# Attention activations and outputs turned by transposing transfers, and the early heads of a long convolution reordered, in a one-core decoder layer

## The reference, cut to what matters

```python
# 1: attention with quantized linear layers (16 heads of 32)
def _act_quant(x):
    s = 127.0 / jnp.clip(jnp.max(jnp.abs(x), axis=-1, keepdims=True), 1e-05)
    return jnp.clip(jnp.round(x * s), -128.0, 127.0) / s
...
qkv = _bitlinear(_layernorm(x), w_qkv)
attn = softmax(causal(einsum('bnhd,bmhd->bhnm', q, k) * SCALE))
x = x + _bitlinear(einsum('bhnm,bmhd->bnhd', attn, v), w_proj)
# 2: long convolution per head (32 heads of 8 channels), gated by ctx
kv = vr[:, :, :, None, :] * x2r[:, :, None, :, :]
y = irfft(rfft(kv, n=2 * L) * k_f)[..., :L] + kv * skip
x = x + einsum('bhijl,bhil->bhjl', y, x1r)
# 3: gated feed-forward on fp8-rounded weights
x = x + down(silu(gate(ln(x))) * up(ln(x)))
```

## Time and profile before

| | |
|---|---|
| median of 3 runs | 1532.92 us (1530.36 to 1533.33) |
| profiled execution | 1535.45 us, its span 1533.7 us |
| PE, DVE, POOL, ACT busy share of the span | 93%, 85%, 74%, 49% |
| attention in steady state | about 123 to 419 us |
| heads 0 to 4 | 494.9 to about 600 us |
| convolution and feed-forward together | from about 610 us |

### The profile page before, as it was taken

One profiled execution on the slowest core, in us unless ns is written; L12 is line 12 of the kernel. 1 busy time (PEld: TensorE's weight loads), 2 busy tenths in 40 slices (PEclk: granted clock), 3 DMA queues, 4 the chain that ended last, 5 costly groups with the idle time before them and its releaser, 6 DMA issues.

```text
span 1533.7 us, 24061 instructions
## 1 busy us (share of the span) xinstructions
PE 1433.5 (93%) x8717; PEld 808.9 (53%) x8717; DVE 1308.0 (85%) x2018; ACT 745.4 (49%) x1334; POOL 1132.6 (74%) x818
## 2 busy tenths in 40 slices
PE   3589999999986988999999999999999999999998
PEld 2477888788763443444444444444444444444443
DVE  5789999999875789899999999999899999999611
ACT  3589999999884112333233333333333334323231
POOL 2379999999984777767776777767866877777432
PEclk9799999999997999999999999999999999999999
DMA  3555555564613422010201300310220121020000
GB/s 140 140 135 152 146 151 157 139 168 128 155 48 97 149 69 67 23 41 25 72 21 35 83 21 21 81 36 22 55 62 21 38 59 42 18 72 1 7 21 28
DMA packets 89218, 113.12 MB, mean 74 GB/s; under 512 B 38133, under 2 KB 42381, under 8 KB 89101
## 3 DMA queue, kind: packets, MB, share of 16 engines
q1 hardware_dynamic: 88908, 111.45, 26.1%
q10 hardware_dynamic: 192, 0.14, 0.1%
HBM read 50.67 MB, written 19.92 MB: 46 GB/s over the span
## 4 chain that ended last, share of the span: by engine, by line
PE 52%; DVE 26%; issue 8%; ACT 7%; POOL 6%; DMA 1%; DVEq 0%; POOLq 0%; SPq 0%; ACTq 0%
PE gu L745 12%; PE gu L759 10%; PE shared_bank L690 6%; DVE y L1110 6%; DVE z L1112 4%; POOL pL L1606 2%; PE y L709 2%; PE y L706 2%; DVE fu L1131 2%; PE y L714 2%; PE y L715 2%; DVE kv L1080 2%; PE gu L704 2%; PE y L712 2%; DVE blockmax L874 2%
## 5 line engine op out<-in xcount | busy, mean ns | idle before, releaser
L1492 ACT ACTIVATE shared<-shared_bank 128x512 f32<-128x512 f32 x162 | 96.6, 596 | 422.6 <-PE shared_bank L690 422.6
L1110 DVE TENSOR_TENSOR y<-shared,y 128x512 f32<-128x512 f32 x324 | 223.9, 691 | 6.8 <-PE y L715 1.2
L1606 POOL TENSOR_TENSOR pL<-pT,pH 128x768 f16<-128x768 f32 x128 | 216.6, 1694 | 12.8 <-ACT pH L1319 5.3
L1732 POOL TENSOR_TENSOR fuL<-fu,fuH 128x512 f16<-128x512 f32 x96 | 121.1, 1262 | 115.9 <-ACT fuH L1507 115.9
L1116 DVE TENSOR_REDUCE oT<-z 128x64 f32<-128x512 f32 x256 | 175.6, 686 | 8.8
L745 PE MATMUL gu<-fT,wu 128*128 128x512 f16 x768 | 183.0, 381 | 0.0
L745 PE MATMUL gu<-fT,wg 128*128 128x512 f16 x768 | 181.4, 379 | 0.0
L1112 DVE TENSOR_TENSOR z<-y,cT 128x512 f32<-128x512 f32 x236 | 162.4, 688 | 11.9 <-PE y L704 6.3
L1678 POOL TENSOR_TENSOR kv<-vT,cT 128x1024 f32<-128x1024 f32 x70 | 148.5, 2123 | 6.9 <-ACT vT L1485 5.5
L759 PE MATMUL gu<-wd,fuH 128*128 128x512 f16 x384 | 145.5, 379 | 0.0
L759 PE MATMUL gu<-wd,fuL 128*128 128x512 f16 x384 | 145.5, 379 | 0.0
(11 more groups left out here) (208 smaller groups left out, 3529.7 us busy)
## 6 DMA issues: line engine op xcount, KB each, us to landing
pack<-qkhl SPq DMA_DIRECT2D x256, 128.0 KB, 2.4
x_sb<-in_x SPq DMA_DIRECT2D x16, 512.0 KB, 4.3
c_sb<-in_ctx SPq DMA_DIRECT2D x32, 256.0 KB, 3.5
hankel<-in_L_xattn_k SPq DMA_DIRECT2D x32, 256.0 KB, 4.0
out_y<-yo SPq DMA_DIRECT2D x32, 256.0 KB, 2.8
x_grp<-x_scratch SPq DMA_DIRECT2D x30, 256.0 KB, 3.5
x_scratch<-x_sb SPq DMA_DIRECT2D x14, 512.0 KB, 2.8
wraw<-in_L_attn_w_qkv SPq DMA_DIRECT2D x3, 1024.0 KB, 9.8
```

What stands on the lines that cost most here:

```text
L1110: chain.step(V.tensor_tensor(bank[:], shared[2 * part + half][:], bank[:], op))
L1606: G.tensor_tensor(pL[n % 2][:], pT[n % NP][:], pH[n % NP][:], ALU.subtract).then_inc(low_done, 1)
L1732: G.tensor_tensor(fuL[ib][:], fu[n % 2][:], fuH[:, ib, :], ALU.subtract).then_inc(f_fl, 1)
```

## The change

Three things change.

1. From batch 2 on, ACT casts the rounded input to bfloat16 in SBUF (`cast_x`, two of 128 x 512) and SP turns it with two transposing transfers into `xqT`. The eight PE transposes and the two copies out of PSUM go.
2. For batches 0 to 13, ACT casts the rounded attention output (`cast_out`) and SP turns it with two transposing transfers (`turn_out`) into `oqT`. The second cast writes into the first half of `o_sb` itself, since its position tile 0 has been read by then. DVE's L914 of the next batch now waits for both transfers to have landed (`o_is_read`).
3. In the convolution heads 0 to 4 take the row order 0, 2, 1, 3 too, heads 1 to 3 turn the former head's result back at s = 4 in place of 2, and the statistics and shift of the next head move from k = 1 and 2 to k = 0 and 1 on DVE and POOL.

The input's arrival is also signalled on four semaphores in place of eight.

```diff
+        xq16 = q("xq16", [P, NT, C], BF16)
...
+        oq16 = [q("oq16", [P, C], BF16), o_sb[:, 0, 0:C // 2].bitcast(BF16)]
...
-        OUT_ROUND_AT, OUT_TURN_AT, OUT_COPY_AT, OUT_AT, X1_AT = (4, 5), (6, 7), (7, 8), (10, 11), (11, 12)
+        OUT_ROUND_AT, OUT_CAST_AT, OUT_TURN_AT, OUT_AT, X1_AT = (4, 5), (5, 6), (6, 7), (10, 11), (11, 12)
...
-        X_ROUND_AT, X_TURN_AT, X_COPY_AT = (6, 7), (8, 9), (9, 10)
+        X_ROUND_AT, X_CAST_AT, X_TURN_AT = (6, 7), (7, 8), (8, 9)
+        X_TURNED_FROM, O_TURNED_TO = 2, B - 2
...
+        def o_is_read(w, b):
+            if b < O_TURNED_TO:
+                for t in range(NT):
+                    w.wait_ge(o_turned[t], 16 * (b + 1))
+            else:
+                w.wait_ge(oqT_pe, NT * (b - O_TURNED_TO + 1))
...
         def row_of(h, s):
-            return SHARED_ROWS[s // 2] if h >= SHARED_FROM else s // 2
+            return SHARED_ROWS[s // 2]
...
+        def back_at(h):
+            return 4 if h < GROUP else 2
...
                 elif k == 1:
                     chain.wait()
                     w.wait_ge(o_sum, b + 1)
                     if b > 0:
-                        w.wait_ge(oqT_pe, 2 * b)
+                        o_is_read(w, b - 1)
                     V.tensor_tensor(o_sb[:, :, 0:C].rearrange("p t (h d) -> p t h d", d=D), oraw[b % 2][:, :, :, 0:D], rl.unsqueeze(3).broadcast_to([P, NT, HEADS, D]),
                                     ALU.mult).then_inc(o_mult, 1)
...
             def prepare(h, k):
-                if k == 1:
+                if k == 0:
...
-                elif k == 2:
+                elif k == 1:
...
+            def cast_x(b, t):
+                w.wait_ge(xround_done, NT * b + t + 1)
+                if b > X_TURNED_FROM:
+                    w.wait_ge(x_turned, 16 * NT * (b - X_TURNED_FROM))
+                S.activation(xq16[:, t, :], xn[:, t, 0:C], ACT.Copy, bias=-ROUND).then_inc(x_cast, 1)
+
+            def cast_out(b, t):
+                w.wait_ge(o_round, NT * b + t + 1)
+                if b > 0:
+                    for i in range(NT):
+                        w.wait_ge(o_turned[i], 16 * b)
+                if t > 0:
+                    w.wait_ge(o_cast, NT * b + t)
+                S.activation(oq16[t][:], o_sb[:, t, 0:C], ACT.Copy, bias=-ROUND).then_inc(o_cast, 1)
...
+            def turn_x(b, t):
+                w.wait_ge(x_cast, NT * (b - X_TURNED_FROM) + t + 1)
+                if b >= 3:
+                    w.wait_ge(v_pe, 2 * (b - 2))
+                Y.dma_start(xqT[b % 3][:, :, t * P:(t + 1) * P], xq16[:, t, :], transpose=True).then_inc(x_turned, 16)
+
+            def turn_out(b, t):
+                w.wait_ge(o_cast, NT * b + t + 1)
+                if b > 0:
+                    w.wait_ge(proj_pe, out_count(b - 1, t))
+                Y.dma_start(oqT[:, :, t * P:(t + 1) * P], oq16[t][:], transpose=True).then_inc(o_turned[t], 16)
...
             for t in STEPS:
                 for b, k in batches(t, FINISH, 14):
+                    if b < O_TURNED_TO and k in OUT_TURN_AT:
+                        turn_out(b, OUT_TURN_AT.index(k))
                     if b < B - 2 and k == X1_AT[1]:
                         store_x1(b)
                 for b, k in project_steps(t):
                     if k == 7:
                         pack_qk(b)
                 for b, k in batches(t, NORM_AT, LOAD_AHEAD + 11, 2):
+                    for i in range(NT):
+                        if k == LOAD_AHEAD + X_TURN_AT[i]:
+                            turn_x(b, i)
                     if k == 0:
                         load_x(b)
```

More of the change, by code:

```diff
@@ L301, in out_count, with x_is_turned, x_is_read, o_is_turned @@
             return 2 * b + t + 1 if b < B - 2 else 2 * (B - 2) + 2 * t + b - (B - 2) + 1
-        X_ROUND_AT, X_TURN_AT, X_COPY_AT = (6, 7), (8, 9), (9, 10)
+        X_ROUND_AT, X_CAST_AT, X_TURN_AT = (6, 7), (7, 8), (8, 9)
+        X_TURNED_FROM, O_TURNED_TO = 2, B - 2
         V_AT, V_SPLIT_AT = (13, 15), (14, 16)
+        def x_is_turned(w, b):
+            if b < X_TURNED_FROM:
+                w.wait_ge(xqT_done, 2 * b + 2)
+            else:
+                w.wait_ge(x_turned, 16 * NT * (b - X_TURNED_FROM + 1))
+        def x_is_read(w, b):
+            if b < X_TURNED_FROM:
+                w.wait_ge(xqT_pe, 2 * (b + 1))
+            else:
+                w.wait_ge(x_cast, NT * (b - X_TURNED_FROM + 1))
+        def o_is_turned(w, b, t):
+            if b < O_TURNED_TO:
+                w.wait_ge(o_turned[t], 16 * (b + 1))
+            else:
+                w.wait_ge(oqT_done, NT * (b - O_TURNED_TO) + t + 1)
+        def o_is_read(w, b):
+            if b < O_TURNED_TO:
+                for t in range(NT):
+                    w.wait_ge(o_turned[t], 16 * (b + 1))
+            else:
+                w.wait_ge(oqT_pe, NT * (b - O_TURNED_TO + 1))
         def pair(t, lag):
@@ L354, in projected @@
         def projected(w):
-            w.wait_ge(xqT_pe, 2 * B)
+            x_is_read(w, B - 1)
+            x_is_turned(w, B - 1)
             w.wait_ge(cbc_pe, B)
@@ L576, in turn_oq @@
                 w.wait_ge(o_round, NT * b + t + 1)
-                bank = misc1.take(("oqT", b, t), w, (oqT_done, 2 * b + t + 1))
+                bank = misc1.take(("oqT", b, t), w, (oqT_done, NT * (b - O_TURNED_TO) + t + 1))
                 for cb in range(CB):
@@ L645, in tensor_program @@
                 for b, k in batches(t, NORM_AT, LOAD_AHEAD + 11, 2):
-                    for j in range(2):
-                        if k == LOAD_AHEAD + X_TURN_AT[j]:
-                            turn_xq(b, j)
                     if k == LOAD_AHEAD + 9:
@@ L774, in tensor_program @@
                         mix_shared(h, s)
-                if g == MIX_STEPS or (s == 2 and 1 <= h < M_HEADS):
+                if g == MIX_STEPS or (1 <= h < M_HEADS and s == back_at(h)):
                     turn_back(h - 1)
@@ L1345, in finish @@
                     S.activation(c2, step, ACT.Copy, scale=ws[:, 5:6]).then_inc(c2_done, 1)
-                copy_at = NEXT_COPY_AT if b == B - 2 else OUT_COPY_AT
-                if k in copy_at:
-                    copy_oqT(b, copy_at.index(k))
+                if b < O_TURNED_TO:
+                    if k in OUT_CAST_AT:
+                        cast_out(b, OUT_CAST_AT.index(k))
+                elif k in NEXT_COPY_AT:
+                    copy_oqT(b, NEXT_COPY_AT.index(k))
             def copy_oqT(b, t):
-                w.wait_ge(oqT_pe, 2 * b + t + 1)
-                if b > 0:
-                    w.wait_ge(proj_pe, out_count(b - 1, t))
+                w.wait_ge(oqT_pe, NT * (b - O_TURNED_TO) + t + 1)
+                w.wait_ge(proj_pe, out_count(b - 1, t))
                 src = misc1.of["oqT", b, t][:].rearrange("p (c n) -> p c n", c=CB)
@@ L1452, in scalar_program @@
                         diagonal(b)
-                    for j in range(2):
-                        if k == LOAD_AHEAD + X_COPY_AT[j]:
-                            copy_xqT(b, j)
+                    for i in range(NT):
+                        if k == LOAD_AHEAD + X_CAST_AT[i]:
+                            cast_x(b, i)
                     if k == LOAD_AHEAD + 10:
```

26 lines of the change are left out of this document (13 added, 13 removed).

## The result

The changed kernel takes 1578.97 us in the median (1576.77 to 1586.68, four runs), the kernel before 1532.54 us on the same chip: 1.0314 times as long, 95% interval 1.0275 to 1.0353. The forecast was slower, at 1557 us. The sign and the place are right; of 46 us, 24.5 were forecast.

A forecast was written before the change was run, and what follows sets the result against it. Attention has PE, ACT and POOL each 97% busy, with POOL limiting PE's relief; late stage is PE-bound. 1535.45 + 29 stall + 2 clock - 7 early heads = 1559.5 us profiled, median 1557, range 1536 to 1580.

The forecast's parts named there:

- The stall's cause: Attention: output transposes issue on SP behind 16 pack transfers, L914 of the next batch waits for them; 29.0 us late.
- The loop: Attention, one SP store to the next: 27.3 us a batch in place of 24.8; last loop 26.0.
- store to issue of the second output transpose: SP's part of the loop: 0.49 to next issue, turn_x 1.31, 16 pack transfers 11.10, first output transpose 1.31 us.
- issue to L947: Second output transpose from issue to landing: 2.4 us, 4.1 at worst.
- L947 to next store: DVE's part of the loop: 10.66 us, not shrinking since DVE is 97% busy in it.
- the clock: PE idle about 3 us a batch; a 1 us slow-clock loss fits in the spare time; +2 us in all.
- rival 2: PE becomes the bound after each stall, by its clock: 1573 to 1590 us, chance 0.12.
- Batch 1: Attention: second transpose lands at 149.0 against L914 at 147.49, 1.5 us late; no store or turn_x delays its pack.
- Rival 3: Stall real but half the size: transposing issues of 0.64 us, loop 26.0 us, total 1542 us; chance 0.13.
- PE's relief: Attention: 16 PE transposes a batch go, 2.4 us beside POOL; taken as 0, at most 4 us gain.
- The heads: Early convolution heads: PE's waits could go; heads 1 to 4 gain 3.8, 1.7, 0.7, 0.8; -7 us, ends -2 and -12.
- the late heads: Late convolution heads: row order stays, only statistics move; PE waited 6.7 us in 820; taken as 0, -2 to +2.

The follow-up runs named there:

- run 3: Changed kernel with one pack issued in two halves, so SP reaches both output transposes behind 8 pack transfers, not 16: 1525.42 us, 0.9953 of the kernel before.
- run 7: The kernel of run 6 with a separate buffer for the second output cast, so L947 waits for the casts alone: 1523.08 us, 0.9927 of the kernel before.
- run 11: Kernel before with the convolution's edits alone, measured on the same chip as run 12: 1523.62 us, 0.9934 of the kernel before.
- run 9: Changed kernel with 64 idle matmuls ahead of the row_max after each of 12 stalled L947: 1565.49 us, 1.0205 of the kernel before.
- run 6: Changed kernel with all inputs turned on PE and copied by ACT as before, outputs still by transposing transfers: 1550.22 us, 1.0104 of the kernel before.
- Runs 5: Changed kernel with outputs turned on PE and copied by ACT as before, inputs still by transposing transfers: 1527.75 us, 0.9957 of the kernel before.
- run 1: Kernel before with the changed convolution alone (row order, later turn_back, earlier statistics and v_sb): 1525.5 us, 0.9949 of the kernel before.
- run 12: The kernel of run 7 again, measured beside run 11: 1523.14 us, 0.9927 of the kernel before.
- Run 10: Kernel before with statistics and v_sb one step earlier, row order and turn_back as before: 1525.98 us, 0.9943 of the kernel before.

## Why the prediction was right or wrong, point by point

**The stall's cause: right.** Late transposes behind the pack, and L947 behind them. Run 3 removes it by order and brings back 54 us; run 7 removes it by a buffer and brings back 27 us (1550.2 to 1523.1), down to where run 11 is without any transposing transfer in the attention.

**The loop: right without its two surprises.** Means over the ten loops from the store at 164.61 to that at 463.17, read from SP's and DVE's instructions as above, beside the same ten of other runs:

| us | forecast | changed kernel | run 9, clock 1.00 | run 6 (forecast) |
|---|---|---|---|---|
| store to issue of the second output transpose | 14.21 | 14.98 | 15.10 | 13.29 (12.90) |
| issue to L947 | 2.4 | 3.04 | 2.66 | 3.00 (2.4) |
| L947 to next store | 10.66 | 11.83 | 10.38 | 10.83 (10.66) |
| sum | 27.3 | 29.86 | 28.13 | 27.13 (26.0) |

**The step that failed is the clock**: "1 to 2 us are to spare and one such loss fits in. I take +2 in all". It didn't fit in. PE, idle for 2.8 to 5.9 us until the maximum, starts again at the lower level and has to finish the first projection before DVE's first L965 can run, so the slow start lies on the loop's own path, each time. That is the mechanism of rival 2, which had 0.12. The granted clock costs 1579.0 - 1565.5 = 13.5 us by the medians of run 9, and 15.6 by each kernel's distance from the kernel before on its own chip (46.4 and 30.9); in the profiles the last term of the loop is 1.45 us longer than at full clock (11.83 against 10.38), 14.5 over ten loops.

Both sides of the estimate were off. The reserve was read against the second L932, at 282.20. The first one, which needs the first projection, stands 3.84 us earlier; the earlier trace rows leave it out:

```profile
278.36 0.74 DVE L932 SCALAR_TENSOR_TENSOR x_sb<-misc,osmall,x_sb 128x512 f32<-128x512 f32 x1
```

```profile
276.78 1.03 PE L587 MATMUL misc<-wprojT,oqT 128*128 128x512 bf16 x4
```

The projection ends at 277.81, 0.55 us before DVE takes it, and in run 6 at full clock the reserve is the same 0.55 (208.86 and 209.41). The loss was put at 1 us, seen after one wait in head 1. From PE's restart to the first work behind this projection it was 4.45 us here (365.73 to 370.18) against 2.30 in run 6 (206.39 to 208.69), a loss of 2.15 us. Less the reserve that is 1.6 us, and DVE's wait at L965 is 1.67.

**The other terms were taken at their medians.** This is the second term that was too small. With the clock at 1.00 the loop is still 28.1: SP's 19 issues take 0.9 us more than in the rows that the forecast added up, and the landing 0.26 more. (DVE's stretch, which was not to shrink, is 0.28 shorter.) The earlier trace rows had it: issues of 1945 ns against 598, landings of 4.1 against 2.4. One such straggler among 19 issues in a serial chain delays the chain by its full length. In the changed kernel the transpose from L1864 has the same spread:

```profile
L1864 SPq DMA_TRANSPOSE oqT<-o_sb x14: 1191/1212/2160, 148.9 to 518.0; - x14
...
  DVE o_sb L947: 49.1, 12
...
DMA to landing us min/median/max: 2.4/2.4/4.2
```

In run 9 the loops are 10 x 0.83 = 8 us longer than forecast by this. In the profile of the changed kernel the two terms are 0.77 and 0.64 us over the forecast, 14 us in ten loops, as much as the clock took there. What makes an issue or a landing a straggler wasn't tried and stays open.

**Batch 1: 4.8 us late, not 1.5.** Batch 0's L947 starts at 125.12 and not at 122.89: the first input transposes hold SP ahead of pack 1 (69.95 against 67.40). Runs 5 and 6 bear that out: with the inputs' transfers alone it starts at 124.70, with the outputs' alone at 121.74. The prediction looked at SP only in the steady state. The pack ahead of batch 0's output transposes then starts at 136.54 and not at 134.32, 2.2 us, and the second transpose lands 3.4 us after its issue and not 2.4 (148.92 to 152.31), another 1.0; together 3.3 us with the rest.

**Rival 3, half the stall.** It wanted transposing issues at 0.64 us. They take 1.19 us at the least and 1.21 to 1.24 at the median (L1858 and L1864). Before, it was 1.19 at the least and 1.26 at the median for the 28 transfers of L1907 that the earlier trace rows don't show, so "1.25 at the least" was true of one half only. "TRN2 transpose DMAs are as fast as regular DMAs" (the Trainium skill, Advanced Engine Details and Errata, X-Bar Transpose) agrees with the landings of 2.4 us and doesn't with the issues, and here the issues were the price (run 6).

**PE's relief: right.** Nothing that shows once the stall is gone (run 3 against 1, run 12 against 11); with the stall it wasn't measured apart. For `Transpose 128x128` the Trainium skill prefers TensorE where a PSUM destination will do (VectorE: DVE Perf Modes, Rules for kernel authors). Runs 11 and 12 differ by 0.5 us, so once the stall is out of the way these runs see neither gain nor loss.

**The heads: the sum nearly right, by luck, and the places wrong.** ACT copies the Toeplitz blocks of one head after the other. Before:

```profile
L1385 ACT ACTIVATE toep<-hankel x32: 617/628/631, 468.6 to 1383.3; 128x512 f32<-128x512 f32 x32
```

After:

```profile
L1435 ACT ACTIVATE toep<-hankel x32: 617/628/631, 530.1 to 1434.7; 128x512 f32<-128x512 f32 x32
```

From the first to the last it was 914.7 us and is 904.6: 10.1 less, where -7 was forecast. To the sixth copy (581.56 before, 638.08 after) it is 5.0 less, so the other 5.1 come later. The next interval, head 4, got longer, from 29.51 to 31.64 (0.8 less was forecast), and the rest, for which the prediction took 0, got 7.2 us shorter. A stretch of four late heads went from 123.27 us to 122.35. The third of them before:

```profile
796.00:825.59 29.59, 29.13 (x110) 13.49 (x109) 28.82 (x42) 10.39 (x19) 21.65 (x16) 1.00 0.10 27
```

and after:

```profile
851.83:880.70 28.87, 28.87 (x110) 13.59 (x109) 28.12 (x43) 10.61 (x20) 21.43 (x16) 1.00 0.09 28
```

PE's waits of the earlier trace rows, 6.7 us, are down to one of 0.4. The prediction read these rows and dismissed them for being 6.7 of 820 us; but PE is the bound there, with 99.5%, so these waits were time of the kernel: 6.3 us of them went, and 7.2 us of time. Heads 1 and 2, from copy to copy, in answer to the earlier trace rows:

```profile
575.35:593.83 18.48, 18.48 (x53) 8.77 (x52) 18.10 (x26) 2.52 (x4) 15.78 (x13) 1.00 0.25 78
593.83:618.62 24.79, 21.60 (x53) 10.19 (x52) 23.44 (x33) 2.52 (x4) 20.08 (x15) 0.86 0.22 66
```

Head 1 is at 18.5 us with PE busy throughout (19.5 forecast). Head 2 is at 24.8 (19.3 forecast; 20.9 before by the same copies) with the clock at 0.86, and at 21.9 in run 11 (531.90 and 553.76) at 1.00; in both PE waits 3.19 us in it for `v_sb`. So these waits did not all go, as was forecast. Head 3 comes to 19.5 (618.62 to 638.08; 20.5 forecast).

From head 1 to head 4 the copies are 0.5 us closer than before (94.83 to 94.37; in run 11 92.91), where -7 was the forecast; 2.4 us come from the two intervals ahead of head 1 and the rest from the late heads. Run 10 tells which edit does what: with the statistics alone the late heads behind head 4 gain the same 7.2 us, and against it the row order with the later `turn_back` (run 11) gains 3.6 us in heads 1 to 3 and loses 2.7 in head 4.

The waits that are left to PE from 554 to 680 us, in answer to the earlier trace rows:

```profile
PE misc L699 <- ACT v_sb L1527: 3.7, 2, 3.2
PE y L737 <- DVE z L1145: 3.5, 4, 1.4
PE y L737 <- DVE kv L1113: 2.1, 1, 2.1
```

**The account.** For the profiled execution 27 us stand between forecast and measurement (1586.68 - 1559.5). Ten loops of 29.9 between the L947 of batches 1 and 11 in place of 27.3 give 26.1, batch 1 gives 3.3, the last loop 1.8 (27.8 in place of 26.0), the end of part 1 another 1.3; less the 2 us of clock already in the sum and the 3.1 that the heads gave on top. That is 27.4.

## What to carry to other kernels

An instruction put behind a burst on an in-order queue comes late by the burst; before moving work there, add up that queue from one release to the next, and look for the single buffer that makes someone wait for the last of it: another order or another buffer removes the stall whole. Where such a loop makes TensorE idle, ask whether TensorE's next work is itself in the loop, since then the slow clock after the pause can be paid each time round, as in all twelve loops here; and measure the time to spare at the first instruction that waits for that work, not at the last. In a chain that is already serial use means, not medians, and count every idle microsecond of an engine that is at 99% as time of the kernel.

## What the runs showed of the hardware that was not expected

TensorE given 768 matmuls of no use made the kernel 13.5 us faster (1579.0 to 1565.5). The granted clock from 250 to 350 us is 0.91 without them and 1.00 with them.

The length of TensorE's pause alone doesn't decide whether the clock falls. In the changed kernel it fell with all twelve pauses, of 2.8 to 5.9 us. In run 6 four pauses of 2.77 to 3.14 us left it at 1.00 (work begins again at 152.75, 206.39, 367.66 and 449.68), and three of 2.78, 2.97 and 3.88 us did not (395.29, 423.71 and 339.19). In head 2 one pause of 3.19 us went with 0.86 in the changed kernel and with 1.00 in run 11. What else decides wasn't tried and stays open.

L947, always of one shape, took 1.24 to 2.60 us in the changed kernel and 2.19 us at the median in run 3. Its L914 took 1.51 us in the middle of the attention before, with POOL at 98.75 and ACT at 97.58 of 100 us, nearly as busy as in run 3. What sets it is open; it stands in the loop's last term.
